# Second layer of a two-layer kernel: the residual's addition four background steps later, the picks' places in a PSUM bank

## The reference, cut to what matters

```python
x_ssm, res = split(x @ W_in.T)            # 512 channels each
x_ssm = silu(causal_conv4(x_ssm) + b_conv)
B_C = (x_ssm @ W_x.T)[16:]                # 16 states
dt = softplus(x_ssm @ W_dt.T + b_dt)
h = exp(dt * A) * h + dt * B_t * x_t      # for each channel and state, over time
y = (h.sum(-1) + D * x_t) * silu(res)
x = x + y @ W_out.T                       # the residual's addition
logits = layernorm(x) @ router            # softmax, top 2 of 32, for two groups
out = x + experts sorted by token's pick
```

## Time and profile before

| | us |
|---|---|
| median of 3 runs | 4823.72 (4823.07 to 4824.93) |
| the profiled execution, its time | 4822.83 |
| its span in the profile | 4821.0 |
| second layer: first scan to last scan | about 2502 to 4144 |
| one chunk of 64 scans | 102 to 106 |

### The profile page before, as it was taken

One profiled execution on the slowest core, in us unless ns is written; L12 is line 12 of the kernel. 1 busy time (PEld: TensorE's weight loads), 2 busy tenths in 40 slices (PEclk: granted clock), 3 DMA queues, 4 the chain that ended last, 5 costly groups with the idle time before them and its releaser, 6 DMA issues. The chain is left out here.

```text
span 4821.0 us, 59211 instructions
## 1 busy us (share of the span) xinstructions
PE 4269.6 (89%) x19350; PEld 2845.4 (59%) x19350; DVE 3709.2 (77%) x5917; ACT 2521.4 (52%) x4939; POOL 3002.8 (62%) x1908
## 2 busy tenths in 40 slices
PE   5689999999999999998989988989989988599993
PEld 1345566555566555565656566666556666488883
DVE  6887777787778787776128999988999989555677
ACT  1343334344334344333458777777877777255552
POOL 3445545465545455554147888888888889655552
PEclk7899999999999999999999999999999999699997
DMA  4233323333333333332121122121122122596887
GB/s 145 83 105 105 110 88 104 107 104 107 108 96 97 110 99 112 105 102 85 54 85 49 67 78 99 71 74 67 71 82 99 69 69 71 180 254 196 266 278 279
DMA packets 304193, 545.54 MB, mean 113 GB/s; under 512 B 31504, under 2 KB 148496, under 8 KB 294928
## 3 DMA queue, kind: packets, MB, share of 16 engines
q1 hardware_dynamic: 275664, 465.56, 30.0%
q0 software_dynamic: 27648, 75.67, 4.4%
q10 hardware_dynamic: 576, 0.53, 0.1%
HBM read 422.72 MB, written 118.92 MB: 112 GB/s over the span
## 5 line engine op out<-in xcount | busy, mean ns | idle before, releaser
L1528 POOL TENSOR_TENSOR c_dbx<-c_dtx,c_Brep 128x1024 f32<-128x1024 f32 x512 | 1203.0, 2363 | 159.2 <-DVE c_hs L1546 119.0
L876 POOL TENSOR_TENSOR a_kv<-a_rk,a_kv 128x512 f32<-128x512 f32 x512 | 807.3, 1589 | 404.4 <-DMA a_kv<-v_rows 404.2
L1546 DVE TENSOR_TENSOR_SCAN c_hs<-psum,c_carry,c_dbx 128x512 f32<-128x512 f32 x768 | 934.6, 1263 | 56.3 <-ACT psum L1535 41.7
L885 DVE TENSOR_TENSOR_SCAN a_S<-a_decay,a_carry,a_kv 128x513 f32<-128x513 f32 x512 | 792.6, 1548 | 181.6 <-POOL a_kv L876 93.3
L802 POOL TENSOR_TENSOR a_hid_e<-a_hid_e,a_g_rep 128x512 f32<-128x512 f32 x256 | 387.1, 1514 | 772.7 <-ACT a_hid_e L791 590.4
L1535 ACT ACTIVATE psum<-c_dt,c_cols 128x512 f32<-128x512 f32 x1024 | 695.2, 688 | 285.6 <-DVE c_hs L1546 283.6
L1571 PEld LDWEIGHTS psum<-ident,c_hs 128*128 128x128 f32 x4096 | 491.9, 145 | 343.2 <-DVE c_hs L1546 169.7
L1571 PE MATMUL psum<-ident,c_hs 128*128 128x128 f32 x4096 | 596.6, 282 | 87.3 <-DVE c_hs L1546 85.1
L891 DVE TENSOR_TENSOR a_prod<-a_rk,a_S 128x512 f32<-128x512 f32 x512 | 546.4, 1067 | 71.9 <-PE psum L907 71.8
L783 PE MATMUL psum<-a_W_down,a_hid_e 128*128 128x256 f32 x2304 | 550.8, 385 | 54.0 <-POOL a_hid_e L802 29.7
L207 PE MATMUL psum<-a_xT,a_W_up 128*128 128x512 f32 x1152 | 559.5, 616 | 14.7 <-ACT a_hid_e L791 14.6
(11 more groups left out here) (287 smaller groups left out, 6817.4 us busy)
## 6 DMA issues: line engine op xcount, KB each, us to landing
a_kv<-v_rows SPq DMA_DIRECT2D x512, 256.0 KB
a_g_rep<-g_rows SPq DMA_DIRECT2D x256, 256.0 KB, 3.9
c_Brep<-b_rows SPq DMA_DIRECT2D x64, 1024.0 KB, 6.0
d_xs<-sorted_rows SPq DMA_DIRECT2D x320, 128.5 KB
d_w<-results SPq DMA_DIRECT2D x64, 512.0 KB, 11.4
d_w<-in_d_experts SPq DMA_DIRECT2D x32, 768.0 KB
a_xa<-in_L_attn_x SPq DMA_DIRECT2D x16, 512.0 KB, 4.7
v_rows<-a_rv SPq DMA_DIRECT2D x16, 512.0 KB, 3.0
```

Of the source, the lines that this page charges most:

```text
L876: m_kv[g] = pool.mark(nc.gpsimd.tensor_tensor(kv[:, g % NV, 1:C + 1], rk[slot][:, 1, hb, :], kv[:, g % NV, 1:C + 1], ALU.mult))
L885: m_scan[q] = dve.mark(nc.vector.tensor_tensor_scan(S[:, q % NS, :], decay[cq % 2][:, hb, :], kv[:, q % NV, :], carry[:, sq_:sq_ + 1], ALU ...
L1528: m_dbx[g] = m_dbx[g + 1] = pool.mark(nc.gpsimd.tensor_tensor(dbx[:, r:r + 2, :], dtx[slot][:, e, :].unsqueeze(1).broadcast_to([P, 2, C]), ...
L1546: m_scan[q] = dve.mark(nc.vector.tensor_tensor_scan(hs[:, q % NR, :], psum[:, DA + q % ND, :], dbx[:, q % NX, :], first, ALU.mult, ALU.add))
```

## The change

The pause between the output product and the residual's addition is 4 steps longer. The bank that holds the ranks also takes the 16 places (columns 256 to 271): the reduction writes there, the cast reads from there, and the bank is given back by the cast, two background steps later than before by the multiplication. The SBUF buffer c_place is gone.

```diff
-                yield from pause(LAG + 2)
+                yield from pause(LAG + 6)
...
-            ranks = bank[:, 0:TL * NE]
+            ranks, in_room = bank[:, 0:TL * NE], bank[:, TL * NE:TL * NE + TL * Z.picks]
...
-            m = G.freed[i] = dve.mark(nc.vector.tensor_tensor(
+            m = dve.mark(nc.vector.tensor_tensor(
                 at_pick[:, :, :, :], R["onehot"][:, :, :, :],
                 ranks.rearrange("p (r e) -> p r e", e=EX).unsqueeze(2).broadcast_to([P, TL * GR, TOP, EX]), ALU.mult))
             yield
             dve.after(m)
-            m = dve.mark(nc.vector.tensor_reduce(flat(place[:, :, :, :].rearrange("p t g k -> p t (g k)")), at_pick[:, :, :, :].rearrange("p r s e -> p (r s) e"), AX, ALU.add))
+            m = dve.mark(nc.vector.tensor_reduce(in_room, at_pick[:, :, :, :].rearrange("p r s e -> p (r s) e"), AX, ALU.add))
             yield
             dve.after(m)
-            m_done["placed", c] = [dve.mark(nc.vector.tensor_copy(flat(route.to_row[:, c % 2, :, :]), flat(place[:, :, :, :].rearrange("p t g k -> p t (g k)")))), m_xn]
+            m = G.freed[i] = dve.mark(nc.vector.tensor_copy(flat(route.to_row[:, c % 2, :, :]), in_room))
+            m_done["placed", c] = [m, m_xn]
...
-        place, over = sb("place", [P, TL, GR, TOP]), sb("over", [P, NE])
+        over = sb("over", [P, NE])
```

## The result

The changed kernel is slower: median 4885.69 us (4879.2 to 4891.88, 4 runs) beside 4824.33 us of the kernel before on the same chip (4823.07 to 4826.36). The ratio is 1.0124, 95% interval 1.0109 to 1.0140. The prediction was 4808, at most 4828. In the code after, lines behind L1393 have a number one higher: L1546 is now L1547, L1553 L1554, L1567 L1568.

What follows compares the result with a forecast made beforehand. The prediction took DVE to bound the kernel's second stage, PE and POOL close behind. Its terms, -6 (later addition), -8.5 (cast) and -1 (last chunk), sum to -15.5: 4807, or 4808 on the median's scale, chance 0.42; range 4788 to 4828.

Steps and rivals of the forecast that it cites:

- the one that was given, at ACT's second block: Slower rival: copies of transposed rows delay ACT's second block, +20 us there, +15 in all, 4839 us; chance 0.11.
- Part 1: The residual's addition 4 steps (3.3 scans) later: -6 us over fourteen chunks, and -1 us in the last chunk.
- The wait moved to the gate: DVE's wait before the addition moves to the gate's multiplication L1553: 4.3 us for 3.95, 60 to 75 in all.
- DVE's loss at scan 20: After the gate's multiplication, additions and statistics are still to do, so DVE is 0.6 us behind in the chunk.
- The stall at scan 31: First later stall, a scan waiting 1.44 us for ACT's exponential, taken as gone, leaving DVE 0.9 us ahead.
- the term of -0.4 a chunk: Second later stall, behind ACT's table loads and c_xs, leaves 0.4 of 0.9 us; fourteen chunks, -6 us.
- the 1 us given: Last chunk: one indirect DMA falls behind the last c_dbx pair, on which a scan waits 1.13 us; -1 us.
- Part 2: Places in PSUM: the cast no longer waits for POOL, -8.5 us; bank held two steps longer at no cost.
- Rival (e): The cast of the places still waits for POOL: -6 - 1, 4817 us; chance 0.10.
- (a): The wait only moves to the gate, ACT's exponentials stay late: 8 - 8.5 - 1 = -1.5, 4822 us; chance 0.22.
- (b): Both later stalls of scans for ACT's exponentials go: -37 - 8.5 - 1, 4777 us; chance 0.12.
- (c): DVE's wait before the addition vanishes instead of moving: -64.5 - 9.5, 4750 us; chance 0.03.

Runs made afterwards that it cites:

- filled: Changed kernel plus four 128x512 products of no use where TensorE idled ahead of the fourth block's skip term; 4855.97 us, ratio 1.0055 to the kernel before.
- both back: Changed kernel with four background steps taken out of the router, addition still four steps later; 4792.8 us, ratio 0.9957 to the kernel before; again 0.9960.
- router back: Kernel before with the places in the ranks' bank and the router four steps earlier, addition at its old place; 4808.1 us, ratio 0.9962; again 0.9960.
- pause alone: Kernel before with only the pause ahead of the addition 4 steps longer, places still in SBUF; ratio 1.0128.

## Why the prediction was wrong

**The step that failed** is this sentence at the end of the working for one chunk: "From there to the chunk's end I see no second effect that has a row of its own, only the router's small DVE instructions in other places." The prediction said itself that everything behind the addition, ranks included, comes 3.3 scans later. It followed the statistics and the transposes to their new places, and stopped there. What it put at nothing without a reason measured 4.2 us of wait in each chunk, 58.7 us in all. Taken one step further, the same trace had the answer: the ranks' last product ended 3.5 us ahead of a skip term with 2.58 us of idle time in its bracket. Moved by four sums they fall behind it. And the price could have been bounded from PE's rows: from the skip term's start, through three sums, two step-size products, a transpose and the ranks themselves it is 7.0 us at the full clock, as "filled" then measured, of which DVE's scans cover 5. That would have been a slower rival of 2 us a chunk with a place and a price; the one that was given, at ACT's second block, had the wrong place.

**What also went unseen** is the clock, for which the prediction had no term. PE's idle time grows there when the ranks leave it, from 2.58 us to 3.77, the low clock behind it comes in every middle chunk where it came in two of three, and it now slows products that DVE waits for: 23 to 35 us.

**Part 1's other steps.** The wait moved to the gate, as said: 78.4 us where 60 to 75 were given, in 16 instead of 14. DVE's loss at scan 20 was 0.7 us for 0.6. The stall at scan 31 went (-1.0 there, so 1.7 won back for 1.44). Of that, 0.4 should have been left at scan 34 and 0.1 was. (The step before it, 0.6 - 1.44, is -0.84; the prediction took 0.9.) In "both back" 0.9 was left. Against "router back" the term of -0.4 a chunk is there in the middle chunks, but over the whole stretch the -6 us measure at about -2, which can't be told from nothing. The last chunk gained more than the 1 us given: from its first scan to its last it took 95.1 us for 98.3. With the ranks back it takes 98.7, so that gain too comes from the ranks' later place.

**Part 2** was right: the casts fell by 8.9 us where 8.5 were taken, the reduction into PSUM takes 692 ns for 676, and the whole part measures 0.17%, or 8 us, by the timed runs. That the cast waited for POOL shows in nearly all of them: 13 of the 16 casts before end within 0.05 us of the end of a c_dbx product, however long they took (0.18 to 2.68 us). Rival (e) is out. The Trainium skill (SBUF — State Buffer, Who interferes with whom) says that a cast between two SBUF tensors can block on the port pair that VectorE shares with GpSimd. The traces agree: no cast from PSUM took over 0.2 us. The pause alone adds that the gain hangs on the place: with the casts four scans later 14 of 16 weren't held up anyway, so in the changed kernel, that is behind the pause, the bank part is worth hardly anything (1.0124 and 1.0128).

**Of the rivals**, (a) has +0.6 us a chunk and the forecast -0.4; up to scan 34 it is -0.1, between the two. (b) fell: the wait at scan 34 is still there. (c) fell as argued. None had the count's wait, so 0.13 for slower was too little, and the range ended 58 us too low.

**What stays open**: why two steps more cost as they do. The idle time, the half clock behind it and the late exponentials at scans 32 to 39 are in its profile, but the one test of it didn't fill the idle time. Open is also by which wait the router's four earlier steps bring their 7 us of stretch (1628.4 to 1621.2).

## What to carry to other kernels

When a step in an engine's queue is moved, follow everything that hangs on it to the end of the chain, and ask of each product not only when its inputs are ready but what blocking instruction it is moved past; a queue runs in order, so a product behind a wait for DVE inherits that wait, and hands it back to DVE. Pin the chain's far end first (here by taking as many steps out behind the moved one as were put in) and only then judge the move. And read the idle time that a moved product leaves behind as a price too: here 3.77 us of nothing in TensorE, ahead of work that the busiest engine waits for, cost more than 3.6 us of useless products.

## What the runs showed of the hardware

- TensorE's granted clock often was at 1.2 GHz behind idle times of 1 to 4 us, and one length didn't always give one outcome. The four products of the fourth block's skip term, over the middle chunks of all 13 profiles: behind 0.25 to 0.85 us of idle time they took 1.16 us in all of 45 cases; behind 1.06 to 1.58 us in 13 of 23; behind 2.2 to 2.6 us in 28 of 50; behind 2.9 us and more never, in 38 cases (1.82 to 2.08 us). What decides in the middle ranges isn't shown.
- Useless products in that gap raised the clock of the stretch behind it from 0.50 to 1.00 and made the kernel 0.7% faster.
- A cast of 16 columns from SBUF to SBUF took 0.15 us where no GpSimd product ran beside it (thirteen in "pause alone"), up to 2.68 us where one did, and 0.14 to 0.18 us from PSUM, in all eleven kernels that have it there.
